# Denominators of a linear attention kept in rows of heads, and experts ranked with two operations, in a six-block hybrid kernel

## The reference

```python
def _L2_ffn_ref(x, router_w, router_b, expert_w, expert_b):     # 8 experts, top 2
    router_probs = softmax(x @ router_w + router_b)
    top_p, top_i = jax.lax.top_k(router_probs, 2)                # ties go to the lower index
    top_p = top_p / sum(top_p)
    expert_out = einsum('bnd,edc->bnec', x, expert_w) + expert_b
    return einsum('bnk,bnkc->bnc', top_p, take(expert_out, top_i))

def _L3_attn_ref(x, ...):                                        # 16 heads of 32
    q, k = elu(q) + 1, elu(k) + 1
    cos, sin = cos(pos), sin(pos)                                # pos = 1.57 * token / 256
    qkv   = q*cos @ (sum_s k*cos v) + q*sin @ (sum_s k*sin v)
    denom = 1 / (q*cos . sum_s k*cos + q*sin . sum_s k*sin + 1e-5)
    return (qkv * denom) reshaped to 512 channels @ dense_w.T + dense_b
```

## Time and profile before

| | us |
|---|---|
| median of the 3 runs | 235.49 (235.47 to 236.01) |
| the profiled execution, its own time | 237.68 |
| its span on the engines | 235.9 |
| PE busy | 199.7 (85%) |
| DVE busy | 170.5 (72%) |
| ACT busy | 107.6 (46%) |
| POOL busy | 38.8 (16%) |

### The profile page before, as it was taken

One profiled execution on the slowest core, in us unless ns is written; L12 is line 12 of the kernel. 1 busy time (PEld: TensorE's weight loads), 2 busy tenths in 40 slices (PEclk: granted clock), 3 DMA queues, 4 the chain that ended last, 5 costly groups with the idle time before them and its releaser, 6 DMA issues.

```text
span 235.9 us, 6609 instructions
## 1 busy us (share of the span) xinstructions
PE 199.7 (85%) x2832; PEld 134.8 (57%) x2832; DVE 170.5 (72%) x389; ACT 107.6 (46%) x268; POOL 38.8 (16%) x54
## 2 busy tenths in 40 slices
PE   7899888999487978998788878759886987989995
PEld 2477488998487978643263444413323633545994
DVE  2699989689689889695784456689699859667101
ACT  2525986779666776432104270320499602046000
POOL 5923000043032133000002003114300000110000
PEclk9999999999997997999999999988999999999999
DMA  6550542552543520101132230000000080000000
GB/s 201 174 161 3 139 142 79 188 148 78 182 153 101 167 74 7 16 8 27 30 111 92 45 80 0 0 0 0 3 3 0 20 351 3 3 0 0 3 0 22
DMA packets 9389, 16.58 MB, mean 70 GB/s; under 512 B 3414, under 2 KB 5229, under 8 KB 9232
## 3 DMA queue, kind: packets, MB, share of 16 engines
q1 hardware_dynamic: 9216, 15.86, 22.2%
q10 hardware_dynamic: 144, 0.30, 0.3%
HBM read 15.38 MB, written 0.78 MB: 68 GB/s over the span
## 4 chain that ended last, share of the span: by engine, by line
DVE 33%; PE 31%; DMA 17%; ACT 8%; issue 5%; POOL 4%; POOLq 0%; SPq 0%; DVEq 0%
PE ps L1514 25%; DMA indexb<-index_rows 16%; POOL arena L573 2%; DVE arena L1408 2%; DVE arena L1405 2%; DVE onehot L1039 2%; ACT indexb L674 2%; PE ps L1801 2%; PE ps L1802 2%; DVE arena L442 1%; DMA cst<-in_cst 1%; POOL rstd L566 1%; DVE att L1091 1%; DVE comp L1372 1%; ACT indexb L629 1%
## 5 line engine op out<-in xcount | busy, mean ns | idle before, releaser
L1514 PE MATMUL ps<-table,onehot 128*128 128x64 bf16 x1728 | 54.7, 196 | 9.0 <-DVE onehot L1039 8.3
L1514 PEld LDWEIGHTS ps<-table,onehot 128*128 128x128 bf16 x1728 | 54.0, 100 | 10.5 <-ACT arena L689 7.4
L1514 PE MATMUL ps<-spare 128*128 128x512 bf16 (+1 forms) x187 | 51.1, 400 | 8.0 <-ACT onehot L629 2.7
L1514 PEld LDWEIGHTS ps<-spare 128*128 128x128 bf16 x187 | 16.7, 104 | 31.9 <-issue 4.6
L689 ACT ACTIVATE arena<-ps 128x512 f32<-128x512 f32 (+1 forms) x40 | 21.8, 550 | 17.6 <-PE ps L1514 17.2
L1039 DVE TENSOR_SCALAR onehot<-indexb,cst 128x2304 bf16<-128x2304 bf16 (+1 forms) x32 | 23.0, 748 | 6.9 <-DMA indexb<-index_rows 6.5
L1514 PE MATMUL ps<-arena 128*32 128x66 f32 (+5 forms) x380 | 22.7, 255 | 2.0 <-DVE arena L1408 1.5
L442 POOL TENSOR_TENSOR arena<-arena,w4p 128x288 f32<-128x288 f32 x18 | 13.9, 803 | 61.0 <-DVE arena L442 61.0
L1514 PEld LDWEIGHTS ps<-arena 128*32 128x32 f32 (+2 forms) x380 | 19.6, 136 | 4.9 <-DVE arena L1408 2.0
L566 POOL TENSOR_TENSOR rstd<-var_eps,cst 128x4 f32<-128x4 f32 (+2 forms) x9 | 8.8, 983 | 80.1 <-DVE var_eps L917 45.4
L629 ACT ACTIVATE indexb<-comp 128x128 bf16<-128x128 f32 x6 | 1.9, 309 | 27.9 <-DVE comp L929 27.9
(11 more groups left out here) (289 smaller groups left out, 338.7 us busy)
## 6 DMA issues: line engine op xcount, KB each, us to landing
indexb<-index_rows SPq DMA_DIRECT2D x21, 384.0 KB, 3.9
arena<-in_toep SPq DMA_DIRECT2D x1, 2120.5 KB, 8.2
l<-in_l SPq DMA_DIRECT2D x1, 646.5 KB
onehot<-lin_split SPq DMA_DIRECT2D x6, 96.0 KB
stu_fq<-in_stu SPq DMA_DIRECT2D x1, 560.0 KB, 3.8
table<-stu_split SPq DMA_DIRECT2D x7, 70.0 KB, 2.0
l<-in_l SPq DMA_DIRECT2D x1, 384.0 KB, 5.8
l<-in_l SPq DMA_DIRECT2D x1, 342.0 KB, 3.0
```

The source lines that it names most:

```text
L1514: return nc.tensor.matmul(out_ap, lhsT, rhs, start=start, stop=stop)
```

## The change

Two edits, and what they need.

1. Ranking: one subtraction of all pairs (lj - li), then one comparison with a constant `ahead`, which is -2^-125 where j stands before i and 0 elsewhere: the difference is above it where lj is larger, or equal with j before i. `ahead` is made once at the front of DVE's list, after the wait for `cst`.
2. Denominators: the rows of heads stay as they are. DVE multiplies bank 4 by rows of cos and sin (`cs_rows`), PE adds the cos and sin rows of each image and splits tokens into two sets of 16 rows (h = 0 and 1), by eight fp32 matmuls on 32 rows and 32 columns; DVE adds 1e-5 and takes the reciprocal, 128x128, once for all. `expand(i, j)` then makes two 128x512 results by 4 + 4 fp32 matmuls of 128 columns, each on one image's 32 rows of the array, by matrices of ones (`heads_of`). i now means one image and two groups hg. The matrices and `cs_rows` come by 20 new DMAs on SP, issued after y1 and before the wait for kv3. `output(i)` now does its two matmuls for one image and two groups, so both write the same 64 rows.

Gone are ACT's copies expand, dc, dp0 and dp1, the transposes, the split into parts on DVE, POOL's memset of `den_p`, and ten fillers of which six waited for DVE; four fillers are new.

```diff
-        expandb, den_parts = late_b[:, 12288:12288 + DH], late_b[:, 12800:12800 + T * P]
-        den_ch, oc = late[:, 6912:6912 + N], late[:, 7936:7936 + 2 * N]
-        den, den_p = late[:, 4096:4096 + T * NHEAD], late_b[:, 2 * 4224:2 * 4224 + T * P]
+        heads_of, cs_rows = [late[:, 4096 + h * DH:4096 + (h + 1) * DH] for h in range(NH)], late[:, 6144:6144 + N]
+        den_cs, den, oc = late[:, 6912:6912 + N], late[:, 7168:7168 + P], late[:, 7936:7936 + 2 * N]
+        head_sum = sb("head_sum", [P, 3 * NHEAD])
+        image_and_pair = lambda i: (i // 4 * 2 + i % 2, i // 2 % 2)
 SP
+            sp.wait_ge(v4.sem, v4["y1"])
+            for b in range(B):
+                first, second = (slice((2 * b + s) * NHEAD, (2 * b + s + 1) * NHEAD) for s in range(2))
+                sp.dma_start(cs_rows[first, :], turn_d[0:NHEAD, 0:N]).then_inc(d_den, 16)
+                sp.dma_start(cs_rows[second, :], turn_d[D:D + NHEAD, 0:N]).then_inc(d_den, 16)
+                sp.dma_start(heads_of[0][first.start:second.stop, :], turn_d[2 * NHEAD:4 * NHEAD, N:N + DH]).then_inc(d_den, 16)
+                sp.dma_start(heads_of[1][first, :], turn_d[NPART:NPART + NHEAD, N:N + DH]).then_inc(d_den, 16)
+                sp.dma_start(heads_of[1][second, :], turn_d[0:NHEAD, N:N + DH]).then_inc(d_den, 16)
             sp.wait_ge(t5.sem, t5["kv3"])
             sp.dma_start(toep, toep_d).then_inc(d_toep, 16)
 POOL
-                    nc.gpsimd.memset(den_p, 0.0).then_inc(g0.sem, g0.step("denz"))
 ACT
-            copy(expandb, turns["expand"], a5, "expand")
-            copy(den_ch, ps[:, 4, 0:N], a5, "dc")
-            for half in range(2):
-                copy(den_parts[:, half * BANK:(half + 1) * BANK], psb[0][:, 0:BANK], a5, f"dp{half}")
 DVE
+            nv.tensor_scalar(ahead[:], c["lt8"], -2.0 ** -125, None, ALU.mult).then_inc(v0.sem, v0.step("ahead"))
...
-                nv.tensor_tensor(out=tee(gt), in0=lj, in1=li, op=ALU.is_gt).then_inc(v4.sem, v4.step(f"rgt{q}"))
-                nv.tensor_tensor(out=tee(eq), in0=lj, in1=li, op=ALU.is_equal).then_inc(v4.sem, v4.step(f"req{q}"))
-                nv.tensor_tensor(out=eq3, in0=eq3, in1=c["lt8"]..., op=ALU.mult)
-                nv.tensor_tensor(out=gt, in0=gt, in1=eq, op=ALU.add).then_inc(v4.sem, v4.step(f"rsum{q}"))
+                nv.tensor_tensor(out=tee(eq), in0=lj, in1=li, op=ALU.subtract).then_inc(v4.sem, v4.step(f"rdiff{q}"))
+                dve.wait_ge(v4.sem, v4[f"rdiff{q}"])
+                nv.tensor_tensor(out=by_tile(gt), in0=by_tile(eq), in1=ahead[:]..., op=ALU.is_gt)
...
+            nv.memset(head_sum[:], 0.0).then_inc(v5.sem, v5.step("headz"))
+            nv.tensor_tensor(out=head_sum[:, NHEAD:2 * NHEAD], in0=c["fold"][:, 0:NHEAD], in1=c["fold"][:, NHEAD:2 * NHEAD], op=ALU.add)
+            dve.wait_ge(d_den, 5 * B * 16)
+            dve.wait_ge(t5.sem, t5["den"])
+            nv.tensor_tensor(out=den_cs, in0=ps[:, 4, 0:N], in1=cs_rows, op=ALU.mult).then_inc(v5.sem, v5.step("dcs"))
+            dve.wait_ge(t5.sem, t5["dsum"])
+            nv.tensor_scalar(den, ps[:, 5, 0:P], 1e-5, None, ALU.add).then_inc(v5.sem, v5.step("deps"))
+            nv.reciprocal(den, den).then_inc(v5.sem, v5.step("dinv"))
 PE
+            pe.wait_ge(v5.sem, v5["dcs"])
+            for b in range(B):
+                rows = slice(b * 2 * NHEAD, (b + 1) * 2 * NHEAD)
+                for h in range(NH):
+                    ins = mm(ps[rows, 5, 0:P], head_sum[rows, (1 - h) * NHEAD:(3 - h) * NHEAD], den_cs[rows, h * P:(h + 1) * P],
+                             start=h == 0, stop=h == NH - 1)
+            ins.then_inc(t5.sem, t5.step("dsum"))
+            occupied(4, 2)
+            pe.wait_ge(v5.sem, v5["dinv"])
+            def expand(*which):
+                for k in range(2):
+                    for h in range(NH):
+                        at, done = (k * NH + h) * P, []
+                        for i in which:
+                            b, pair = image_and_pair(i)
+                            rows, hg = slice(b * 2 * NHEAD, (b + 1) * 2 * NHEAD), 2 * pair + k
+                            done.append(mm(ps[:, EB[i % len(EB)], at:at + P], heads_of[h][rows, hg * P:(hg + 1) * P], den[rows, :]))
             def output(i):
-                for b in (2 * half, 2 * half + 1):
-                    n, rows = hg * B + b, slice(b % 2 * 2 * D, (b % 2 + 1) * 2 * D)
+                for hg in (2 * pair, 2 * pair + 1):
+                    n = hg * B + b
-            expand 0 to 3, to_rows(1), expand 4, expand 5
+            expand(0, 1)
+            expand(2, 3)
+            expand(4, 5)
             output(0)
             output(1)
-            expand(6)
-            expand(7)
+            expand(6, 7)
             output(2)
             output(3)
```

More of the change, by code:

```diff
@@ L326, in hybrid @@
                    + " "
[L327 removed]
+                   + "headz heads dcs deps dinv "
                    + " ".join(f"qn{i}" for i in range(8)) + " oc0 x50 oc1 x51")
[L329 to L330 removed]
+        a5 = Steps(sem("scalar_linear"), "pm0 pd0 s1a s2a pm1 pd1 " + " ".join(f"ek{t} vc{t}" for t in range(T))
+                   + " eq0 eq1 eq2 eq3 kv0 kv1 eq4 eq5 eq6 eq7 kv2 kv3")
         t5 = Steps(sem("tensor_linear"), "st0 k0 v0 k1 v1 st1 " + " ".join(f"k{t} v{t}" for t in range(2, T))
[L332 to L333 removed]
+                   + " q0 q1 q2 q3 kv0 kv1 q4 q5 q6 q7 kv2 kv3 den dsum "
+                   + "ex0 ex1 ex2 ex3 ex4 ex5 ex6 ex7 out0 fold0 out1 fold1")
         tw = Steps(sem("tensor_weights"), "wd0 wd1 wd2 wd3 m1 m2 l1 l2 sel s1 s2")
@@ L1427, in _ @@
                              op=ALU.add).then_inc(v5.sem, v5.step("bias"))
[L1429 to L1439, removed]
-                for h in range(NH):
-                    dve.wait_ge(v5.sem, v5[f"cos{half}{h}"])
-                    nv.scalar_tensor_tensor(out=dn[:, :, h, :], in0=dt[:, :, h, 1, :], scalar=c["cs"][:, 2 * h + 1:2 * h + 2],
-                                            in1=dn[:, :, h, :], op0=ALU.mult, op1=ALU.add)\
-                        .then_inc(v5.sem, v5.step(f"den{half}{h}"))
-                dve.wait_ge(v5.sem, v5[f"den{half}1"])
-                nv.reciprocal(dv, dv).then_inc(v5.sem, v5.step(f"inv{half}"))
-                dve.wait_ge(v5.sem, v5[f"inv{half}"])
-                for part, name, less in ((0, f"dh{half}", f"dr{half}"), (1, f"dm{half}", f"ds{half}")):
-                    nv.tensor_copy(dp[:, :, part, :], dv).then_inc(v5.sem, v5.step(name))
-                    dve.wait_ge(v5.sem, v5[name])
-                    nv.tensor_tensor(out=dv, in0=dv, in1=dp[:, :, part, :], op=ALU.subtract).then_inc(v5.sem, v5.step(less))
-                    dve.wait_ge(v5.sem, v5[less])
-                nv.tensor_copy(dp[:, :, 2, :], dv).then_inc(v5.sem, v5.step(f"dl{half}"))
@@ new lines, in _ @@
+            nv.memset(head_sum[:], 0.0).then_inc(v5.sem, v5.step("headz"))
+            dve.wait_ge(v5.sem, v5["headz"])
+            nv.tensor_tensor(out=head_sum[:, NHEAD:2 * NHEAD], in0=c["fold"][:, 0:NHEAD], in1=c["fold"][:, NHEAD:2 * NHEAD], op=ALU.add)\
+                .then_inc(v5.sem, v5.step("heads"))
+            dve.wait_ge(d_den, 5 * B * 16)
+            dve.wait_ge(t5.sem, t5["den"])
+            nv.tensor_tensor(out=den_cs, in0=ps[:, 4, 0:N], in1=cs_rows, op=ALU.mult).then_inc(v5.sem, v5.step("dcs"))
@@ L1879, in _ @@
             pe.wait_ge(v5.sem, v5["ksb"])
[L1881 to L1885, removed]
-                for i in range(4):
-                    t = 4 * half + i
-                    ins = nc.tensor.transpose(psb[0][:, i * P:(i + 1) * P], den_p[:, t * P:(t + 1) * P], identb[:])
-                ins.then_inc(t5.sem, t5.step(f"dp{half}"))
             for hg in range(HG):
```

66 lines of the change are left out of this document (23 added, 43 removed).

## The result

| | us |
|---|---|
| kernel after, median of 20 runs | 233.99 (231.60 to 236.79) |
| kernel before, median of 20 runs beside them | 237.68 (234.46 to 241.83) |
| ratio after / before | 0.9868, 95% interval 0.9829 to 0.9908 |
| profiled execution of after: own time, span | 233.97, 232.2 |

The change makes the kernel 1.3% faster (0.9% to 1.7%), some 3.1 us. The forecast was 2.8 us off 235.49, 1.2%. The level under it was low: the 20 runs of the kernel before, of which the first three are a part, have a median 2.2 us above that of those three. Ratios compare only executions within 1.5% of the fastest of their kernel, which is why they aren't quotients of the medians.

What follows compares the result with a forecast made beforehand. The bound was taken to be a chain of waits shared nearly equally by DVE and PE. Ranking -1.6, `ahead` +0.13 and denominators -1.3 sum to -2.8 us, from 235.49 to 232.7 us; 8-in-10 range 231.8 to 234.1.

Steps and rivals of the forecast that it cites:

- The level: Whole kernel: the forecast differences were added to a median of 235.49 us for the kernel before.
- Ranking, -1.6: Experts' ranking on DVE: each of two halves goes from 2.28 to 1.49 us, -1.6 us in all.
- The worry about PE's fillers: Behind the ranking: PE's fillers move less than DVE and might delay the transposes; given 0 to 0.2 us, taken as 0.0.
- rival 4: Ranking: PE's fillers or POOL's share hold the next transposes back, -0.8 instead of -1.6, total 233.5 us; 6 in 100.
- ahead, +0.13: Front of DVE's list: one 128x64 tensor_scalar ahead of POOL's tap matrices adds 0.13 us.
- Denominators, -1.3: End of the linear attention: fold starts at 200.75 instead of 202.06, -1.3 us, with PE as the bound.
- POOL's memset "followed by nothing for long", 0: Removed memset on POOL: costed at nothing, since nothing follows it for long.
- DMAs on SP, 0: 20 new DMAs behind y1: 0.59 us an issue, 11.8 us in all, ended by 175.4; costed at nothing.
- Rival 1: Denominators: matmuls start only in program order, so they bring -0.2 to -0.3, total 233.8 us; 12 in 100.
- Rival 2: Expansion: PE's idle gaps bring a stretch at the lower clock, costing 1.7 us, total 234.4 us; 9 in 100.
- Rival 3: Expansion: row tiles don't run side by side, PE needs 3.6 us more ahead of fold, total 236.3 us; 5 in 100.

Runs made afterwards that it cites:

- e9: The kernel before, unchanged, run against itself: ratio 1.0034 (0.9981 to 1.0086).
- e10: The kernel after, unchanged, run once more: ratio to before 0.9819 (0.9696 to 0.9941).
- e11: The kernel after with fold(0) put ahead of output 6, run a second time: ratio to before 0.9773 (0.9686 to 0.9859).
- e1: The kernel before with the new ranking alone, `ahead` included: ratio to before 1.002 (0.9967 to 1.0072); logits to rmax 2.96 us.
- e2: The kernel after with the old ranking, so the denominators alone: ratio to before 0.9935 (0.9874 to 0.9996).
- e3: The kernel before with POOL's memset of den_p moved behind DVE's step bias: rmax to keys 14.26 us instead of 14.65.
- e6: The kernel after with fold(0) put ahead of output 6: ratio to before 0.9791 (0.9728 to 0.9854); denominators' stretch 0.80 us shorter.
- e7: The kernel after with the first four expansions ordered by image: 48 records in 4.03 us instead of 2.61; denominators' stretch 15.26 us.
- e4: The kernel after with a same-size POOL memset, of a tile nobody reads, where the old one stood: rmax to keys 14.65 us.
- e8: The kernel after without the four fillers between the sums and the first expansion: denominators' stretch 18.59 us, 4.80 more.
- e5: The kernel after with all expansions on image 0's row tile: 48 records in 7.12 us; denominators' stretch 24.14 us against 13.79.

## Why the prediction was right or wrong

- **The level: wrong, and this is the step that failed.** "I add the differences to the median" took the 235.49 us of three executions for the level of the kernel before. The median of the twenty is 237.68, 2.2 us more. The three are all among the five lowest of the twenty; whether that is the luck of the draw or the kernel really ran faster at that moment is open. Beside the later experiments the kernel before had medians of 239.20, 238.06 and 238.77. From the measured level the forecast change gives 237.68 - 2.8 = 234.9 us, and the measured ratio gives 237.68 x 0.9868 = 234.5, both above the top of my range, 234.1, which allowed nothing for the level. The measured median, 233.99, is 1.3 us above the forecast of 232.7. It lies inside the range only because a second error cancels a part of the first: the change was forecast too small, 2.8 us against 3.1 by the ratio, 3.3 by the traces and 3.7 between the medians. That is luck. The warning stood in my own rows: the profiled execution of the kernel before took 237.68.
- **Where the scatter is.** The table has 148.3 to 156.9 us for the first logits. The largest share of the chain between 20 and 150 us is the DMA of index rows, 23% to 43% of it in the five executions for which I read it (before, after, e9, e10, e11). Of the four executions under 151, e1, e2 and e3 show the full clock until their logits, and e11 one short stretch at the lower level; all the others show two or more. What sets the one and the other in an execution was not tried.
- **Ranking, -1.6: right.** 4.55 to 2.95. The worry about PE's fillers (0 to 0.2 us) was void: in after PE is idle 1.89 us ahead of them instead of 2.69, the clock doesn't fall there, and the transposes start at 164.61, 0.06 after DVE's last write for them. In e6 and e7 the clock did fall there (0.50 from 156 to 159), and rmax to keys was 14.26 all the same. So rival 4, a gain held back by the fillers or by POOL, is out too.
- **ahead, +0.13: right in size,** 0.10. From DVE's first operation on cst to the statistics of x it is 0.52 us (4.12 to 4.64), 0.42 before, and to POOL's tap matrices 2.05 instead of 1.95, in every execution with and without it.
- **Denominators, -1.3: right,** -1.35, by terms that mostly came out: dcs to E, the start of the expansion, 2.66 us (2.5 forecast; dsum and its hand-over took 0.76 and the last hand-over 0.15), E to fold 7.39 (7.65). The three pairs were a little faster: the pair (4, 5) overlapped the end of the ones before, so DVE's seventh multiplication didn't wait, and the eight ended at E + 6.04 instead of 6.3. PE, not DVE, was the bound, as worked out.
- **POOL's memset "followed by nothing for long", 0: wrong,** -0.4 us. This is the term that the change was short of. I looked at who waits for the memset and not at what runs beside it. The row was in the timeline: a cast of 0.62 us among five of 0.23. e3 and e4 show the cause from both sides.
- **DMAs on SP, 0: right.** They were issued from 162.29 to 172.2, mostly 0.46 us apart and not 0.59, and toep's issue came with kv3, at 185.26. ACT's copy of `expandb`, 0 too: right (e3 and e4).
- **Rival 1, strict order: out in its full form.** dsum took 0.66 for 16 records; but e7 shows that work on another tile starts only a few records ahead of its turn.
- **Rival 2, the clock: didn't occur in five executions of the new stretch with its fillers** (after, e2, e4, e7, e10), nor in the two with fold early, and its price was put too low. e8 shows 4.8 us, not 1.7, since the low level outlasted the expansions and the outputs too.
- **Rival 3, tiles not side by side: out.** Its price, 3.6 us, fits the records of e5 at the full clock (0.11 each); with the fall of the clock, which it left out, e5 lost 10.35.

Taken together: -1.60 - 0.41 - 1.35 + 0.10 = -3.26 us, or 1.4% of 237.68, inside the measured interval.

## What to carry to other kernels

Before a time is forecast to within 1%, look at how executions of the unchanged kernel differ and where: here the part up to the first logits scattered by 8.6 us, one stretch behind it by 1.6, and the rest by less than 0.1, so stretches between marks of a single trace told 0.1 us where twelve timed runs didn't tell 1.6. A level taken from three executions needs a margin of its own in the range. Of an operation that goes away, look at what runs beside it on the other engines, not only at who waits for it: one row longer than its sisters is the sign. When work moves onto row tiles of the matrix engine, put neighbours in program order on different tiles (e7), keep the engine occupied ahead of it (e8), and place the consumer that others wait for (here fold) ahead of work that nobody waits for yet.

## What the runs showed of the hardware

- fp32 matmuls on 32-row tiles of different rows run side by side: 48 records in 2.61 us (after), where 34 on one tile took 3.76 (e5).
- They run ahead of program order by little: image 1's first record started when 13 of the 16 records of image 0 ahead of it had started (e7), the third pair's when 26 of 32 had (after).
- The granted clock can fall while PE is busy without a gap: in e5 it stood at 1.00, then at 0.50, in one unbroken run of 48 such records. After 1.52 us idle it fell within the first 0.5 us of the same work on two tiles (e8), and with four fillers in that gap it stayed at 1.00 in seven executions. I had thought of idle time alone.
- A cast of 128x128 takes 0.23 us on DVE (e3), 0.62 beside a memset on POOL (before); a tensor_tensor of the same size is not held up, 0.29 beside the same memset.
